# A two-stage cross-attention and mixture-of-experts kernel: keys and values of all batches first, queries last

## What is computed

```python
x = x + xattn0(layernorm(x), ctx, ctx, mask)     # 16 heads of width 16, masked
x = x + ffn0(layernorm(x))                       # self-attention, then 8 experts 256 -> 1024 -> 256, top 1
x = x + xattn1(layernorm(x), ctx, ctx)           # cross-attention with biases, no mask
x = x + ffn1(layernorm(x))                       # 256-way gate, expert = index mod 8, 256 -> 256
```

## Time and profile before

| | us |
|---|---|
| median of 3 runs | 1180.72 |
| lowest and highest run | 1171.85, 1183.11 |
| the profiled execution | 1175.31 |
| its span, first to last instruction | 1173.5 |

### The profile page before, as it was taken

The page is one execution under the profiler, slowest core; times in us unless marked ns, Lnnn a source line. Parts: engine busy times, 40 slices in busy tenths (PEclk is TensorE's granted clock), DMA queues, the critical chain, the costliest instruction groups (busy, mean ns, idle before and its releaser), DMA issues. The chain is left out here.

```text
span 1173.5 us, 18594 instructions
## 1 busy us (share of the span) xinstructions
PE 1046.4 (89%) x6202; PEld 570.2 (49%) x6202; DVE 726.5 (62%) x1804; ACT 614.3 (52%) x1305; POOL 221.8 (19%) x360
## 2 busy tenths in 40 slices
PE   7989999999899899999967999996989999998380
PEld 4532333333364334444466999994533444446360
DVE  4767787877478798889370000005679988856632
ACT  2236666666622587777713444431337877784250
POOL 2000000000110214153302222211001111021255
PEclk9969999999999799999967999998979999999695
DMA  9954433330049332421286855625964332302164
GB/s 301 322 151 115 110 92 74 91 74 2 2 186 312 69 82 57 100 69 35 88 343 224 318 184 177 187 70 175 324 181 109 80 90 67 69 15 72 27 180 143
DMA packets 76878, 157.51 MB, mean 134 GB/s; under 512 B 9261, under 2 KB 26289, under 8 KB 75377
## 3 DMA queue, kind: packets, MB, share of 16 engines
q1 hardware_dynamic: 72704, 146.09, 41.6%
q0 software_dynamic: 4080, 10.23, 3.3%
HBM read 102.03 MB, written 52.17 MB: 131 GB/s over the span
## 5 line engine op out<-in xcount | busy, mean ns | idle before, releaser
L960 ACT ACTIVATE r<-ps 128x512 f32<-128x512 f32 x768 | 418.0, 600 | 189.1 <-PE ps L1074 188.4
L411 DVE TENSOR_REDUCE m<-ps 128x1 f32<-128x512 f32 x512 | 321.0, 683 | 49.0 <-PE ps L1043 49.0
L1074 PE MATMUL ps<-stacks 50*128 50x512 f32 x768 | 286.0, 463 | 8.3 <-DMA stacks<-mT 5.0
L1043 PE MATMUL ps<-stacks 48*128 48x512 f32 x720 | 288.1, 477 | 3.7 <-DVE r L488 3.0
L1074 PEld LDWEIGHTS ps<-stacks 50*128 50x128 f32 x768 | 122.0, 191 | 183.6 <-ACT r L960 125.7
L1083 PE MATMUL ps<-r 128*32 128x512 f32 x1536 | 209.8, 619 | 1.6 <-ACT r L960 1.6
L407 DVE CUSTOM_DVE_ANT_0 r<-ps,r 128x512 bf16<-128x512 f32 x256 | 166.0, 688 | 54.0 <-PE ps L1043 53.3
L1731 DVE TENSOR_TENSOR r<-ps,r 128x256 f32<-128x256 f32 x46 | 19.5, 425 | 194.6 <-PE ps L1779 167.6
L1043 PEld LDWEIGHTS ps<-stacks 48*128 48x128 f32 x720 | 117.7, 193 | 24.4 <-DVE m L411 14.6
L886 POOL CAST mparts<-m 128x16 fp32r<-128x16 f32 x48 | 9.8, 205 | 554.1 <-DVE m L411 318.6
L1695 ACT ACTIVATE r<-ps,b1c 128x128 f32<-128x128 f32 x184 | 52.5, 368 | 94.0 <-PE ps L1761 94.0
(11 more groups left out here) (149 smaller groups left out, 1034.9 us busy)
## 6 DMA issues: line engine op xcount, KB each, us to landing
r<-in_w SPq DMA_DIRECT2D x31, 1024.0 KB, 6.0
stacks<-q_parts SPq DMA_DIRECT2D x96, 192.0 KB, 3.6
stacks<-k_parts SPq DMA_DIRECT2D x96, 192.0 KB, 4.5
k_parts<-r SPq DMA_DIRECT2D x24, 512.0 KB, 3.6
q_parts<-r SPq DMA_DIRECT2D x24, 512.0 KB, 4.3
k_parts<-r SPq DMA_DIRECT2D x24, 256.0 KB, 4.2
q_parts<-r SPq DMA_DIRECT2D x24, 256.0 KB, 3.7
r<-in_ctxT SPq DMA_DIRECT2D x8, 512.0 KB, 5.1
```

The costliest lines, as they stand in the source:

```text
L411: ins = dve.tensor_reduce(out, mem.ps[:, bank, :], AX.X, ALU.max)
L960: act.activation(mem.probs[:, u // HG, u % HG, :], ps[:, ST + unit_of(b, g, u) % DEEP, :], ACT.Exp, scale=SCALE).then_inc(a.p_exp.sem, 1)
L1043: pe.matmul(ps[:, led_bank(n), :], stack_of(mem.qst[g], h, ROWS)[:, t * P:(t + 1) * P], stack_of(mem.kst[g], h, ROWS), start=True, stop=Tr ...
L1074: pe.matmul(ps[:, ST + N % DEEP, :], stack_of(mem.kst[g], h, KROWS)[:, kt * P:(kt + 1) * P], stack_of(mem.qst[g], h, KROWS), start=not a.m ...
```

## The change

The two cross-attentions get functions of their own (`cross_tensor`, `cross_scalar`, `cross_vector`, `cross_gpsimd`, `cross_sync`); the self-attention keeps `project_*`. In a cross-attention

- values and keys of all four batches come first, then the queries of all four batches. The eight key products and eight query products are 16 items that take turns over four part buffers and four PSUM banks (1 to 4). The values leave PSUM by ACT, and in `xa1` POOL adds their bias when it copies a group.
- the early scores stand behind the last four query products, four behind each, in two PSUM banks (0 and 6). The stacks of the first two groups are loaded when the queries of batch 0 are stored.
- `xa1` has its operands in `r2`; its contexts 0 and 1 and its key and value weights are loaded at the end of the self-attention. PE does the values of batch 0 and its first key product between the two products of the routing, its second key product and the values of batch 1 behind them, and the other keys and values behind the last expert. DVE does the rests of batch 0's keys behind the routing.
- after the first mixture DVE sums batch 0 alone; POOL sums the other three, between its scales.
- the second expert weights move to `r1` and are loaded in 16 pieces during the self-attention; the first expert weights move to `r2`. The semaphores of `xa0` are cleared during the self-attention.
- the rows of ones beside the stacks are written by two DMAs in place of eight. PE no longer waits for DVE's last sum behind the experts of `me0`.

The core of the diff (blank lines left out):

```diff
+    banks = CROSS_EARLY if a.cross else EARLY
     for v in range(EACH * i, EACH * (i + 1)):
         if v == 0:
-            pe.wait_ge(a.hT_ready.sem, a.hT_ready.at(B))
+            if not a.cross:
+                pe.wait_ge(a.hT_ready.sem, a.hT_ready.at(B))
+            pe.wait_ge(a.v_ready.sem, a.v_ready.at(B))
             pe.wait_ge(a.stacks[0].sem, 64)
             if a.fresh:
-                pe.wait_ge(a.shift_ones.sem, 16 * SIDES * NG)
+                pe.wait_ge(a.shift_ones.sem, 16 * SIDES)
                 pe.wait_ge(a.preset.sem, 4)
-        if v == 2:
-            pe.wait_ge(a.v_ready.sem, a.v_ready.at(B))
-        if v >= len(EARLY):
-            pe.wait_ge(a.s_max.sem, v - len(EARLY) + 1)
+        if v >= len(banks):
+            pe.wait_ge(a.s_max.sem, v - len(banks) + 1)
         h, t = led_tile(v)
-        pe.matmul(mem.ps[:, EARLY[v % len(EARLY)], :], stack_of(mem.qst[0], h, ROWS)[:, t * P:(t + 1) * P],
+        pe.matmul(mem.ps[:, banks[v % len(banks)], :], stack_of(mem.qst[0], h, ROWS)[:, t * P:(t + 1) * P],
...
+BUFFERS = 4
+TURNED = (5, 7)
+PART_BANK = (2, 3, 4, 1)
+CROSS_EARLY = (0, 6)
+def value_bank(b, k):
+    return 0 if k == 0 else 5 if b < 2 else 6
...
+def cross_tensor(pe, a):
+    mem = a.mem
+    ps = mem.ps
+    def values(b):
+        pe.wait_ge(a.c_loaded[b % 2].sem, a.c_loaded[b % 2].at(b // 2, 16))
+        if b:
+            pe.wait_ge(a.v_ready.sem, a.v_ready.at(b))
+        for k in range(2):
+            for t in range(2):
+                for c in range(C):
+                    ins = pe.matmul(ps[:, value_bank(b, k), t * D:(t + 1) * D],
+                                    a.cT[b % 2][:, c, (2 * k + t) * P:(2 * k + t + 1) * P],
+                                    a.w[:, 2, c, :], start=(c == 0), stop=(c == C - 1))
+            ins.then_inc(a.v_ps.sem, 1)
+    def product(item, which, n, src):
+        if item >= BUFFERS:
+            pe.wait_ge(a.r1.sem, item - BUFFERS + 1)
+        for c in range(C):
+            ins = pe.matmul(ps[:, PART_BANK[item % BUFFERS], :], a.w[:, which, c, n * P:(n + 1) * P], src[:, c, :],
+                            start=(c == 0), stop=(c == C - 1))
+        ins.then_inc(a.qk_ps.sem, 1)
+    def keys(b, n):
+        product(key_item(b, n), 1, n, a.cT[b % 2])
+    def queries(b, n):
+        pe.wait_ge(a.hT_ready.sem, a.hT_ready.at(b, C))
+        product(query_item(b, n), 0, n, a.hT[b % 2])
+    def turn_tokens(b):
+        if b:
+            pe.wait_ge(a.hT_ready.sem, a.hT_ready.at(b))
+        pe.wait_ge(a.hn_ready.sem, a.hn_ready.at(b, T))
+        for c in range(C):
+            for t in range(T):
+                ins = pe.transpose(ps[:, TURNED[c], t * P:(t + 1) * P], a.hn[:, t, c * P:(c + 1) * P], mem.ident[:, :])
+            ins.then_inc(a.hT_ps.sem, 1)
+    def all_queries():
+        if a.qo_loaded is not None:
+            pe.wait_ge(*a.qo_loaded)
+        turn_tokens(0)
+        for b in range(B):
+            for n in range(C):
+                queries(b, n)
+                if n == 0 and b + 1 < B:
+                    turn_tokens(b + 1)
+                if b >= B - 2:
+                    early_scores(pe, a, C * (b - (B - 2)) + n)
+    return values, keys, all_queries
...
+    def first_part(item, n, query):
+        at = a.cols + (0 if query else C) + n
+        act.wait_ge(a.qk_ps.sem, item + 1)
+        if item >= BUFFERS:
+            act.wait_ge(a.stored[item % BUFFERS].sem, a.stored[item % BUFFERS].at(item // BUFFERS))
+        act.activation(a.parts[item % BUFFERS][:, 0, :].bitcast(F32R), ps[:, PART_BANK[item % BUFFERS], :],
+                       ACT.Identity, bias=mem.cols[:, at:at + 1]).then_inc(a.hi.sem, 1)
...
+def cross_sync(sp, a):
+    mem = a.mem
+    def context(b):
+        if b >= 2:
+            sp.wait_ge(a.qk_ps.sem, key_item(b - 2, C - 1) + 1)
+        sp.dma_start(a.cT[b % 2][:, :, :], a.dram["ctxT"][b]).then_inc(a.c_loaded[b % 2].sem, 16)
+    def ones_rows():
+        for j in range(SIDES):
+            rows = mem.ones_rows[j * SIDE + ROWS:j * SIDE + KROWS, :].rearrange("r (i n) -> r i n", n=P)
+            sp.dma_start(rows, mem.onesf[:, :].unsqueeze(1).to_broadcast([PARTS, NG * PAIRS * S // P, P]))\
+              .then_inc(a.shift_ones.sem, 16)
+    def parts(item, b, n, query):
+        sp.wait_ge(a.r1.sem, item + 1)
+        out = a.dram["q" if query else "k"][b, n * P:(n + 1) * P, :, :]
+        store_parts(sp, a, item % BUFFERS, out, query)
+    def keys(b, n):
+        parts(key_item(b, n), b, n, False)
+    def all_queries():
+        for b in range(B):
+            for n in range(C):
+                parts(query_item(b, n), b, n, True)
+            if b == 0:
+                for n in range(C):
+                    done = query_item(0, n)
+                    sp.wait_ge(a.stored[done % BUFFERS].sem, a.stored[done % BUFFERS].at(done // BUFFERS + 1))
+                for g in range(AHEAD - 1):
+                    load_stacks(sp, a, 0, g)
+        load_stacks(sp, a, 0, AHEAD - 1)
+    return context, ones_rows, keys, all_queries
...
+        to, v = mem.vg[g % 2][:, :, :, 0:DK], mem.v[:, b, g, :, :].rearrange("p t (h d) -> p t h d", h=HG)
+        if a.cross and a.rows is not None:
+            row = mem.rows[:, a.rows:a.rows + 1, g * GW:(g + 1) * GW].to_broadcast([P, T, GW])
+            pool.tensor_tensor(to, v, row.rearrange("p t (h d) -> p t h d", h=HG), ALU.add).then_inc(a.vg_ready.sem, 1)
+        else:
+            pool.tensor_copy(to, v).then_inc(a.vg_ready.sem, 1)
...
+    for b in range(B - 1):
+        store_rows(sp, m, b)
+    sp.wait_ge(m.acc_stored.sem, m.acc_stored.at(B))
+    sp.dma_start(*keys_values).then_inc(a.kv_loaded[0], 16)
+    store_rows(sp, m, B - 1)
+    sp.wait_ge(m.experts.sem, 1)
+    for s in range(W1_BUFFERS):
+        first_weights(s)
...
+    context(2)
+    for n in range(C):
+        keys(0, n)
+    for s in range(W1_BUFFERS, DEPTH):
+        first_weights(s)
...
+    context(3)
+    all_stored(sp, m)
+    y = m.dram["y"].rearrange("(b t p) d -> b p t d", b=B, t=T)
+    for b in range(B):
+        sp.dma_start(m.yg[:, b * T:(b + 1) * T, :], y[b]).then_inc(m.fetched[b].sem, 16)
+    for n in range(C):
+        keys(1, n)
+    ones_rows()
+    for b in range(2, B):
+        for n in range(C):
+            keys(b, n)
...
+def other_sums(pool, m, b):
+    if b == 1:
+        pool.wait_ge(m.acc_loaded.sem, 16 * B)
+    pool.wait_ge(m.fetched[b].sem, m.fetched[b].at(1))
+    for k in range(2):
+        x = m.mem.x[:, b, 2 * k:2 * k + 2, :]
+        pool.tensor_tensor(x, x, m.yg[:, b * T + 2 * k:b * T + 2 * k + 2, :], ALU.add).then_inc(m.x_added.sem, 1)
...
+        def second_weights(sp, b, g):
+            G = NG * b + g
+            f, some = FT - 1 - G // 2, slice(G % 2 * E // 2, (G % 2 + 1) * E // 2)
+            sp.dma_start(mem.w2[:, f, some, :], w2[:, f, some, :]).then_inc(weights[0], 16)
...
+                statistics, normalise, keys, queries = cross_vector(dve, xa0)
+                dve.wait_ge(weights_a, 32)
+                for b in range(B):
+                    for n in range(C):
+                        keys(b, n)
+                    if b == 0:
+                        dve.wait_ge(x_first, 16)
+                    if b == 1:
+                        dve.wait_ge(x_rest, 16 * (B - 1))
+                    statistics(b)
+                    if b == 0:
+                        normalise(0)
+                for t in range(T):
+                    mask_for_maxima(dve, xa0, 0, t)
+                normalise(1)
+                queries(0, 0)
+                normalise(2)
+                queries(0, 1)
+                queries(1, 0)
+                normalise(3)
+                queries(1, 1)
+                for b in range(2, B):
+                    for n in range(C):
+                        queries(b, n)
+                        early_maxima(dve, xa0, C * (b - 2) + n)
...
+                statistics, normalise, keys, queries = cross_vector(dve, xa1)
+                keys(0, 0)
+                keys(0, 1)
                 expert_vector(dve, me0)
-                start, begin, rest = project_vector(dve, xa1)
-                combine_vector(dve, me0, (start, begin))
-                rest()
+                keys(1, 0)
+                keys(1, 1)
+                keys(2, 0)
+                first_sums(dve, me0)
+                dve.wait_ge(me0.x_ready.sem, 1)
+                statistics(0)
+                keys(2, 1)
+                normalise(0)
+                dve.wait_ge(me0.x_added.sem, me0.x_added.at(1))
+                statistics(1)
+                keys(3, 0)
+                normalise(1)
+                keys(3, 1)
+                queries(0, 0)
+                dve.wait_ge(me0.x_added.sem, me0.x_added.at(2))
+                statistics(2)
+                normalise(2)
+                queries(0, 1)
+                queries(1, 0)
+                dve.wait_ge(me0.x_added.sem, me0.x_added.at(3))
+                statistics(3)
+                normalise(3)
```

(26 more changed lines are left out.)

581 lines of the change are left out of this document (313 added, 268 removed).

## The result

The kernel after takes 1206.43 us (median of 4 runs, 1200.69 to 1212.72), the kernel before 1181.91 in the same series: a ratio of 1.0224, with a 95% interval of 1.0177 to 1.0272. The forecast was 1180.1, with a range to 1197: it is slower by 24.5 us, about 2% (the interval lies on both sides of 2%), beyond the range and on the side of rival A, but farther out than A's 1192.

What follows compares the result with a forecast made beforehand. TensorE, busy 89% of the span, was taken as the bound, its waits winnable. Routing +0.9, first cross-attention +9.2 and second -10.7 gave -0.6 us: from 1180.72 to 1180.1 us, range 1163 to 1197.

Steps and rivals of the forecast that it cites:

- rival A: Early-score rounds of both cross-attentions: clock falls to half, rounds 7.0 us, each stage 6.0 longer, 1192 us; chance 0.25.
- Routing, forecast +0.9: Work added between the routing's two products on PE makes the second product 0.9 us late; bounds +3.8 and -2.3.
- First cross-attention, forecast +9.2: First cross-attention: attention starts at 82.8 us instead of 73.56, 9.2 us later; bounds +3 and +15.
- The fourth context: First stage's fourth context load: lands 5 us after issue, at 31.3, costing 0.8 us; keys end at 38.4.
- The rounds: Early scores with two banks: 5.2 us per round, 18.7 us from first score to last maximum in each stage.
- The tail: From the last early-score maximum to the attention's start: some 6.1 us, against 10.6 and 9.4 before.
- Second cross-attention, forecast -10.7: Second cross-attention: attention starts at 856.3 us instead of 867.02, 10.7 us earlier; bounds -17 and -5.
- The hole: PE's 8.25 us of idleness behind the last expert: filled by 17.6 us of keys and values, to 811.4.
- B: Early-score rounds of both stages: cost nothing new, 3.1 us each as before, 1167.5 us; chance 0.25.

Runs made afterwards that it cites:

- f3: e2 with the second cross-attention's early keys and values moved from the first routing to behind the last expert: 1189.22 us, ratio 1.01 to the kernel before.
- e4: Kernel after, with the first stage's mask load issued behind the fourth context instead of ahead: 1200.34 us, ratio 1.0173 to the kernel before.
- e3: Kernel after, with unused matmuls on TensorE in the stack wait and early-score rounds to hold the clock: 1189.75 us, ratio 1.0073 to the kernel before.
- g3: f5 with the sums of batches 1 to 3 on DVE instead of POOL: 1169.76 us, ratio 0.9913 to the kernel before.
- f5: f1 with, in the second stage, e2's order and f4's placing of batch 0's second query product: 1165.53 us, ratio 0.9896 to the kernel before.
- e1: Kernel after, with four banks instead of two for the early scores of both cross-attentions: 1185.03 us, ratio 1.004 to the kernel before.
- e2: Kernel after, with the last four query products ahead of all sixteen early scores, still two banks: 1183.68 us, ratio 1.0047 to the kernel before.
- f1: Kernel after, with the first cross-attention as in the kernel before, routing and second cross-attention as changed: 1177.14 us, ratio 0.9994 to the kernel before.
- f4: e2 plus e4's mask order and, in both stages, batch 0's second query product before the next token turn: 1175.02 us, ratio 0.9982 to the kernel before.
- g2: The kernel before, unchanged, profiled once more as a control: 83.8 us from the second expert choice to the end.

## Why the forecast was wrong, step by step

*Routing, forecast +0.9:* right within its bounds. The second product of the routing isn't late at all: it stands 8.45 us behind the choice, as in the kernel before (614.74 and 606.29), with the work moved there ahead of it.

```profile
635.75 0.72 PE L1758 MATMUL ps<-r 128*128 128x69 bf16 x16
```

From the first attention's start to the end of the last expert the kernel after is 1.9 us shorter (718.4 against 720.2), and f3 shows what the work moved there is worth: 8 us.

*First cross-attention, forecast +9.2, measured +22.1.* Three terms were too small.
- The fourth context. I let it land 5 us after its issue, as the stores and loads of the earlier trace rows do; it took 8.6 behind 1 MB of mask. PE waited 3.38 us in place of 0.8 and began the values at half clock (5.41 us in place of 3.62), so the keys ended at 43.1 in place of 38.4, and the first early score came at 63.0 in place of 58: +5.0. That the first score follows the end of the keys the seven traces at e4 show; e4 alone, with the context 2.3 us faster, moved the score by 0.25 us only.
- The rounds. "One round = 5.2 us": measured 6.82, so 24.2 us from the first score to the last maximum in place of 18.7: +5.5. This is the step that failed, and it failed as rival A said: the clock was down when the first early score came. e3 measured 5.17 with the clock up. With the second stage it is 10.9 of the 21.3 us by which the two stages missed.
- The tail. 6.1 was worked out for the way of the maxima. In the first stage PE had also the mask to turn and twelve leading scores to do, at half clock; 95.65 has no idle time ahead of it, and PE was busy for 7.75 of the 8.48 us, so this was PE's own work: 8.5, +2.4.

```profile
87.17:95.65 8.48, 7.75 (x25) 3.72 (x23) 6.46 (x22) 2.31 (x3) 0.76 (x3) 0.50 0.94 202
```

*Second cross-attention, forecast -10.7, measured -2.3.* The hole went as forecast, and the keys and values ran at full clock. The first score came at +40.55, not +37.7 (+2.9), because two of DVE's normalisations took 3.3 us beside POOL's additions, 3.8 us more together, and the second query product ran in part at half clock; storing and loading then took 7.9 us in place of 9.2. g3 shows, in f5's order, that DVE would pay the same if it did the additions itself. The rounds cost 5.4 us more, as in the first stage. The tail, 6.3 in place of 6.1, was right. With the rounds repaired (e1, e2) the start is at +61.2 and +62.1: the forecast's 62.5.

*The rivals.* A had the right mechanism, the right place and nearly the right price (7.0 for a round, 6.0 per stage). It got a chance of 0.25, less than the forecast, although a wait of 3 us for the stacks stood in my own list just ahead of the rounds. The Trainium skill (TensorE: Matmul & The Clock Gate, HAM oscillation) holds that compute shorter than the wait for data beside it starts throttled each time. The products did start at half clock in every round of both stages (3.3 to 3.5 us each), but the rounds are not the page's case: beside 5.1 us of PE's work stood a wait of 1.7 us, for DVE's maxima, and not, as the prediction has it, a wait as long as the work. e3, which filled that wait and the one ahead of the first score, had full clock from its second product on. B (rounds that cost nothing new) is what e1 has, by four banks; with two, in this order, it was wrong.

*What the sum hid.* Two large terms of opposite sign left -0.6, and each was wrong by about its own size (+9.2 by 12.9, -10.7 by 8.4), both to the slow side. f1 and f5 tell them apart: the first stage costs some 27 us as made; the second, with the routing, is worth 1% once its rounds are cured. The first stage has no hole to fill (PE, which starts at 7.31, is busy for 37.08 of its first 45 us, and the DMA share is 0.94, and the earlier trace rows): putting all queries last only moves the first stack load back. Even repaired (f4) it starts its attention 8 us later than in f5, and the kernel is 0.9% slower.

## What to carry to other kernels

When buffers are cut in a loop between two engines, look for the heavy instruction that ends up behind the wait for a buffer: it joins the round trip, and its engine idles for the rest of it. Price such a loop at both levels of TensorE's clock; here a wait stood ahead of it, and the lower level was the right one. Moving work into a hole pays where there is a hole; the same order in a stage without one only delays what the next stage waits for. When a sum has two large terms of opposite sign, try each change alone before both.

## What was not expected

A DVE normalisation of four tiles took 3.28 us beside two POOL additions of 2.53 us together, and 1.38 us where none ran (g3). The Trainium skill (SBUF — State Buffer, SBUF: two separate sides) says that GpSimd and some DVE instructions take turns at a shared pair of ports, and that one of them holds it for a whole instruction. The trace agrees: the first two of the four DVE instructions took 1.36 and 1.35 us and each ended 0.15 us behind one of the two additions; the other two took 0.40 us, as all four do in g3 (0.41).

One execution of the same kernel ended its last mixture in 78.9 us, another in 83.8 (g2). A difference of 4 us in a stage that a change doesn't touch should be looked for in a second profile before it is explained; I had counted it against the change in f1's expectation.

The fourth context, 512 KB each time, took from 6.3 to 9.5 us to land, by what was queued ahead of it; and asking for the stacks 8.6 us earlier (f4) brought their first score forward by 6.0, of which 5.6 were the keys' earlier end.
